# Graph network on one core: two of the four window transfers of a hop's group are issued by ScalarE

## What is computed

```python
agg = entity_emb
for _ in range(3):
    h, t = agg[head], agg[tail]
    left = h @ q_w
    right = tanh(rel * t @ k_w)
    att = sum(left * right, axis=1)
    e = exp(att - segment_max(att, head)[head])
    w = e / segment_sum(e, head)[head]
    agg = segment_sum(w[:, None] * rel * t, head) / max(count, 1)
    agg = agg / max(norm(agg), 1e-12)
    out = out + agg + entity_emb
```

## Time and profile before

| what | value |
|---|---|
| median of three runs | 11539.55 us |
| span of the profiled execution, first to last instruction | 11570.2 us |
| first to last product of the first hop (L1806), by its timeline | 3017.9 to 5790.9 us |
| the same of the second hop | 5874.9 to 8633.2 us |
| the same of the third hop | 8726.4 to 11488.3 us |

### The profile page before, as it was taken

How to read it: one execution, slowest core, us unless ns; L and a number is a source line. 1 busy time by engine, 2 the same in 40 slices (tenths; PEclk the granted TensorE clock), 3 DMA queues, 4 the chain that set the end, 5 groups by cost and what they waited for, 6 DMA issues and landing times. The chain is left out here.

```text
span 11570.2 us, 241070 instructions
## 1 busy us (share of the span) xinstructions
PE 8077.2 (70%) x47197; PEld 6146.6 (53%) x47197; DVE 6642.3 (57%) x27980; ACT 6199.6 (54%) x15908; POOL 6401.1 (55%) x6757
## 2 busy tenths in 40 slices
PE   2666666666688888888866666666666666666665
PEld 2444444444466666666645555555554555555554
DVE  4666666665555565655655555555554555555556
ACT  1666666666355555555545555555554555555554
POOL 4566666664455555555545555555545555555553
PEclk8776677767788999999978888888888888888887
DMA  2111111111455555555544444444434444444443
GB/s 68 43 43 43 43 43 42 43 43 41 123 176 176 177 176 176 177 175 176 176 124 139 138 138 138 137 139 136 138 118 134 136 138 137 138 136 136 137 136 112
DMA packets 1180950, 1401.16 MB, mean 121 GB/s; under 512 B 216215, under 2 KB 883640, under 8 KB 1180472
## 3 DMA queue, kind: packets, MB, share of 16 engines
q1 hardware_dynamic: 963734, 951.33, 25.8%
q0 software_dynamic: 216064, 444.28, 14.2%
q10 hardware_dynamic: 876, 2.56, 0.1%
HBM read 888.87 MB, written 183.76 MB: 93 GB/s over the span
## 5 line engine op out<-in xcount | busy, mean ns | idle before, releaser
L622 POOL DMA_INDIRECT tails<-node_rows,idx x4992 | 4715.4, 945 | 3803.9 <-remote 1610.6
L1798 DVE SCALAR_TENSOR_TENSOR acc<-acc,fade,banks 128x129 f32 x4992 | 1741.7, 349 | 2100.6 <-remote 1310.5
L1902 PE MATMUL banks<-rt,weight_t 128*128 128x129 f32 x9984 | 1674.8, 315 | 749.1 <-DVE acc L1798 724.3
L622 POOL DMA_INDIRECT l_rows<-in_x_dram,l_idx x1664 | 1591.9, 957 | 1075.1 <-issue 453.6
L1951 ACT ACTIVATE weight<-att,low 128x128 f32<-128x128 f32 x4992 | 1593.0, 391 | 1058.6 <-DVE low L1822 577.1
L1902 PEld LDWEIGHTS banks<-rt,weight_t 128*128 128x128 f32 x9984 | 1483.3, 223 | 849.8 <-issue 795.8
L1887 PE MATMUL banks<-rtt,k_sb 128*128 128x512 f32 x2496 | 1505.3, 685 | 533.8 <-issue 441.7
L1872 PE MATMUL banks<-right,window 128*128 128x128 f32 x9984 | 1567.3, 307 | 281.8 <-DVE tile_low L1814 163.4
L1814 DVE CUSTOM_DVE_ANT_0 att<-banks,agg 128x128 f32<-128x128 f32 x4992 | 1152.8, 287 | 982.6 <-remote 768.9
L1872 PEld LDWEIGHTS banks<-right,window 128*128 128x128 f32 x9984 | 1430.9, 221 | 358.3 <-DVE tile_low L1814 227.5
L1929 ACT ACTIVATE right<-banks 128x512 f32<-128x512 f32 x1248 | 730.5, 585 | 809.3 <-remote 639.2
(11 more groups left out here) (317 smaller groups left out, 9961.5 us busy)
## 6 DMA issues: line engine op xcount, KB each, us to landing
window<-qt SPq DMA_DIRECT2D x4992, 64.0 KB
agg<-pairs_kept SPq DMA_DIRECT2D x832, 384.0 KB
pairs_kept<-agg SPq DMA_DIRECT2D x416, 384.0 KB
rows_in<-tile_rows SPq DMA_DIRECT2D x208, 512.0 KB
tails<-node_rows,idx POOLq DMA_INDIRECT x4992
l_rows<-in_x_dram,l_idx POOLq DMA_INDIRECT x1664
node_rows<-agg SPq DMA_DIRECT2D x6, 1024.0 KB, 6.0
node_rows<-agg SPq DMA_DIRECT2D x3, 1088.0 KB, 8.2
```

Of the source, the lines that this page charges most:

```text
L622: e.indirect_dma_start(out=rows[:, g, t, :], out_offset=None, in_=of, in_offset=bass.IndirectOffsetOnAxis(ap=idx[:, b, first + t:first + t ...
L1798: e.scalar_tensor_tensor(to, to, fade[:, g2, t:t + 1], bank[b_acc + t // 2][:, t % 2 * WIDE:t % 2 * WIDE + WIDE], ALU.mult, ALU.add).then_ ...
L1902: mm = s.e.matmul(bank[b_acc + t // 2][:, t % 2 * WIDE:t % 2 * WIDE + WIDE], weight_t[:, s.slot(lag, 2), t, :], rt[:, s.slot(lag, RING), t ...
```

## The change

A new function, load_windows, holds the windows' part of the step. It is called by SyncE for tiles 0 and 1 of the group and by ScalarE for tiles 2 and 3, each with its own load of two section numbers and its own wait. In ScalarE's queue it stands right behind the index copy and ahead of all else in the step. The window's semaphore still counts four transfers. ScalarE also waits once per hop, ahead of its loop, until the query table is complete.

```diff
+                def load_windows(s, lag, e_type, first_tile):
+                    if s.live(lag):
+                        g4 = s.slot(lag, UNROLL)
+                        q = load_sections(s, e_type, at_column, (z.sections - 1) * P, lag, first_tile, GROUP // 2)
+                        s.wait_ge((s_att, done(lag + UNROLL)))
+                        for t in range(GROUP // 2):
+                            s.e.dma_start(window[:, g4, first_tile + t, :], qt[:, bass.ds(q[t], P)]).then_inc(s_win[g4].h, 16)
+
                 def sync_hop(s):
...
-                    if s.live(2):
-                        g4 = s.slot(2, UNROLL)
-                        q = load_sections(s, mybir.EngineType.SP, at_column, (z.sections - 1) * P, 2)
-                        s.wait_ge((s_att, done(2 + UNROLL)))
-                        for t in range(GROUP):
-                            s.e.dma_start(window[:, g4, t, :], qt[:, bass.ds(q[t], P)]).then_inc(s_win[g4].h, 16)
+                    load_windows(s, 2, mybir.EngineType.SP, 0)
...
                 def scalar_hop(s):
                     scalar_idx(s, others, idx, s_rt, 2)
+                    load_windows(s, 2, mybir.EngineType.Activation, GROUP // 2)
...
                         scalar_q(e)
+                        e.wait_ge(s_qt.h, s_qt.at(node_groups))
                         pipeline(e, f"ha{hop}", scalar_hop, z.slot_groups, deep + 2, (TURN, GROUP * TURN) if first else (TURN, 2 * TURN, GROUP * TURN), TURN)
```

## The result

The changed kernel takes 11655.37 us (median of 4 runs, 11644.55 to 11665.70) against 11538.52 for the kernel before (4 runs, 11534.21 to 11544.98): ratio 1.0099, interval 1.0084 to 1.0113. That is 117 us slower, where 317 us faster was forecast.

The account below looks back on a forecast made before the run. The prediction took SyncE's lateness, with part of each period left to GpSimd's gathers, as the bound. 1257 us of waits less 624 us exposed on ScalarE gives 633; half, 317, off 11539.55 gives 11223 us, range 10900 to 11880.

Parts of the forecast that it names:

- What bounds the kernel: In the hops, SyncE's queue is late all the time, at 6.69 us per group; part of each period belongs to GpSimd's gathers.
- SyncE's relief, 1.51 us per group: On SyncE's queue, two of four window transfers go, saving 3.03 / 2 = 1.51 us per group.
- The waits that go, 1257 us: ScalarE's waits for the pair load (1040.7 us) and VectorE's for rows_in (216.4 us) can go.
- ScalarE's work, 1.6 us: Added on ScalarE per group: load 0.3 us, two transfers 1.2 us, the rest 0.1 us.
- Half of the net reaches the end: Of 633 us less standing still in the hops, half, 317 us, reaches the end, under 387 us for all bursts of eight.
- Exposed 0.5 us: Ahead of copy_relations, 0.5 of ScalarE's 1.6 us shows per group, 624 us; instructions ahead cover 1.75 us.
- Slower: ScalarE's sequencer is slowed during gathers as SyncE's is: 1.48 us exposed per group, +295 us, 11835 us; chance 0.33.
- The larger gain: SyncE alone bounds the hops, so the period falls by the whole 1.51 us, 1884 us, to 9656 us; chance 0.10.
- No change: Gathers set the hops' period, other waits replace that for the pair, time stays 11540 us; chance 0.12.
- the rule weighed: An issuing engine's track must be solid with DMA slices; SyncE's is about half, so the change gives nothing.
- The signs: In the hops: SyncE waits, ScalarE's pair wait under 200 us, more bursts of eight, transfers near 0.5 us, 0.5 us "issue".
- The signs of being wrong: SyncE never waits, ScalarE's transfers and loads average 0.7 us or more, or TensorE and VectorE wait longer for right and weight_t.

Follow-up runs that it names:

- sync_two: Kernel before, but SyncE issues the windows of tiles 0 and 1 only and nobody the other two: 11411.66 us, ratio 0.9895.
- The halves alone: Kernel before with half of SyncE's windows left out (11411.66 us); kernel before with ScalarE's load and two extra transfers into an unread buffer added (11765.38 us).
- the added waits: Kernel before with always-met waits added on ScalarE, four per group in the trace: 11742.77 us, ratio 1.0015.
- the two transfers: Kernel before with two extra ScalarE transfers per group, fixed columns, no register load, slow speed: 11884.94 us, ratio 1.0168.
- extra_no_load_fourth: Kernel before, all four windows on SyncE, plus two ScalarE transfers of fixed columns without load, slow speed: 11884.94 us, ratio 1.0168.
- extra_again: Kernel before, all four windows on SyncE, plus ScalarE's load and two transfers into a spare buffer, fast speed: 8875.16 us, ratio 1.0000.

## Why the prediction was wrong, point by point

**What bounds the kernel: right that SyncE was late, wrong about what that was worth.** SyncE was late all the time and its lateness ended two waits of 1257 us. `sync_two` shows that behind these waits others stood ready. (11 of the 31 rows were said to exceed 2.5 us; it is 12, which changes little.)

**SyncE's relief, 1.51 us per group: right.** By the measure of the earlier trace rows, first to last transfer, all 1248 groups took 2.97 us in the mean before, and the two that stayed take 1.39, so 1.58 us are gone. The load of two numbers takes longer than that of four (477 against 298 ns in the median), which gives back (547 - 414) / 1248 = 0.11 us.

**The waits that go, 1257 us: right as waits.** 1040.7 fell to 14.4 and 216.4 to 4.2.

**ScalarE's work, 1.6 us: too small.** The durations come to (1245 + 684 + 342) / 1248 = 1.82 us. From the address of the load to the end of the second transfer it is 2.40 us in the mean, the wait included; at the fast speed the same distance is 1.91. So some 0.3 us were missed in the undisturbed price, most of it the load (0.49 against 0.3 us), and up to 0.5 us by the slow instructions.

**Half of the net reaches the end: the step that failed.** It was a chosen factor, with no row behind it but a cap of 387 us. It puts 1257 / 2 = 628 us of gain and 624 / 2 = 312 us of cost at the end of the kernel. The halves alone measured 119 us of gain and 235 us of cost. So the gain was too large by 509 us and the cost, if anything, too large by 77, and together they make nearly all of the miss of 434 us. What the runs showed in its place: a tenth of the waits that vanish reaches the end, 119 of 1257 us, because in ScalarE's queue 386 of 471 us come back as waits for VectorE, TensorE and its own sequencer.

**Exposed 0.5 us: the second step, too small.** "Issue" before copy_relations grew in the second hop from 42.9 / 389 = 0.11 to 488.9 / 386 = 1.27 us, 1.16 us more per group. The cover of 1.75 us was counted at the sequencer's undisturbed pace, and at that pace 0.5 us is about right: it is 0.43 at the fast speed. But at the slow speed the sequencer meets slow instructions in 252 bursts where it met them in 34. With 1.16 in place of 0.5 the prediction's own sum gives (1257 - 1448) / 2 = -95, or 11635 us, close to the 11655 measured. That would have been luck, since neither half of that sum has its measured size. That "issue" here costs time at the end isn't shown by its size either: with the added waits it is 0.38 us per group for 23 us, with the two transfers 0.50 for 192.

**The rivals.** Slower was right in its sign, and its condition held: it decides above 1.0 us exposed per group, and 1.16 was measured (1.48 had been worked out). Its size, +295, is 2.5 times the +117, and it has the same factor of a half, so it too took 628 us of gain for 119. The larger gain fell with `sync_two`: with half of SyncE's windows gone altogether the time is 1.05% less, not 1884 us less. "No change" named what happened to the gain, the other waits taking the pair's place, and missed that ScalarE's added instructions aren't free. As for the rule weighed (the Trainium skill, "Perfetto Trace Analysis", section "What 'DMA-bound' means"), which would not have called SyncE the bound: the trace of `sync_two` is nearer to it than the prediction was. The Trainium skill's "DMA: Bandwidth & Descriptors", section "Issuing engines are not separate DMA queues", says that a second issuer saves sequencer time only; that time was worth at most about 119 us here, traffic included, and moving the transfers cost more on the second sequencer than it saved on the first.

**The signs.** SyncE waits, the pair's wait is gone, the transfers' median is 494 ns, as said. Bursts of eight should have grown and went from 90 to 87 in 6000 to 8600 us, and "issue" before copy_relations was to be 0.5 and was 1.27 us. The signs of being wrong hardly came: SyncE waits, ScalarE's transfers and loads have means of 0.50 and 0.55 us and not 0.7, and TensorE waits longer for right (294.3 us against 89.6) but less for weight_t (38.8 against 205.3). They watched durations, and the loss lies between the starts.

## What to carry to other kernels

Before moving an instruction to another engine's queue, price both halves at the end of the kernel, not as waits: one run with the work taken off the old engine and one with it added to the new one gave -119 and +235, which add up to the result. Such halves also take off or add the traffic, so a third run is needed to split them. A wait that vanishes is worth what the next wait in line leaves of it, here a tenth. And an engine that goes on at normal pace with few instructions doesn't show how it would go with more: "issue" before the copy of the relations was 0.43 us per group at the fast speed and 1.27 at the slow one, for the same program.

## What the runs showed of the hardware that was not expected

- The same program takes 8874 to 8888 us or 11530 to 11720 us. At the slow speed SyncE, ScalarE and VectorE have stretches, in the later part of a burst of gathers and up to 2 us past its end before the change (3 after it), in which instructions begin 0.7 us or twice that behind one another, a register operation as well as a transfer; the slow ones last 0.70 us in the median. The sequencers of TensorE and GpSimd have none: in 6000 to 8600 us no register or wait instruction of theirs exceeds 0.21 us. In the traces at the fast speed the first three have none either: their longest register or wait instruction in the hops is 0.42 us, on SyncE. What sets the speed is open: no edit turned one into the other. It isn't a property of certain chips alone, since one of 19 runs on one chip took 11553 us among 8888, with a granted clock of 0.814 against 0.925.
- The slow stretch comes to ScalarE at about the same count of instructions, whatever they are. From the start of a burst to the first slow register or wait instruction it has, in the median, 17 instructions of its sequencer (25 to 28 with the engine's own) before the change, with the added waits, with the change and with `extra_no_load_fourth` alike. In time that is 6.2 us into a burst before, 5.6 with `extra_no_load_fourth`, 4.6 with the added waits and 3.5 with the change (means), so ScalarE gets there sooner and in more bursts when it has more instructions: 34, 92, 140 and 252 bursts in 6000 to 8600 us. The means of the count scatter more: 28, 27, 24 and 21, the engine's own included. On SyncE it is 9 instructions and 3.1 us before. Which resource stands behind it is open.
- A register load of two numbers took 477 ns (SyncE) and 493 ns (ScalarE) in the median, that of four numbers 298 (SyncE). At the fast speed it is 528 and 490 for two, and 302 for four on SyncE (`extra_again`), so the difference has nothing to do with the slow stretches. A load of four on ScalarE wasn't run.
- ScalarE's transfers have a queue of their own in the profile (q10: 876 packets before, 360300 after), and the DMA engines' mean busy share went from 0.46 to 0.48 and 0.49 in the stages of the second and third hop.
